# Block inverses of a chunked delta rule, cut into four quarters instead of two halves

## The reference

```python
q, k, v = (silu(conv4(x @ W.T)) for W in (Wq, Wk, Wv))
beta = sigmoid(x @ Wb.T)
A = where(tri_strict, -(kb @ k.T), 0)          # kb = k * beta, 32x32 per chunk
T = solve_triangular(eye - A, eye, lower=True)
u, w = T @ v, T @ kb                           # then a scan over the chunks
local = fir3(v), fir15(v), fir63(v)            # per channel filters
o = p0*local_s + p1*local_m + p2*local_l + p3*delta_out + p4*v
```

## Time and profile before

| | |
|---|---|
| median of 3 timed runs | 2339.09 us (2338.53 to 2339.15) |
| the profiled execution, own time | 2325.58 us |
| its span, first to last instruction | 2323.8 us |
| stage 1 (project) | from 0 to 359.2 us of the span |
| stage 2 (weights_fir) | from 359.2 to about 576 us |
| busy share over the whole span | PE 90%, DVE 50%, ACT 37%, POOL 23% |

### The profile page before, as it was taken

How to read it: one execution, slowest core, us unless ns; L and a number is a source line. 1 busy time by engine, 2 the same in 40 slices (tenths; PEclk the granted TensorE clock), 3 DMA queues, 4 the chain that set the end, 5 groups by cost and what they waited for, 6 DMA issues and landing times.

```text
span 2323.8 us, 41398 instructions
## 1 busy us (share of the span) xinstructions
PE 2086.2 (90%) x16936; PEld 1766.6 (76%) x16936; DVE 1157.7 (50%) x1819; ACT 864.5 (37%) x1406; POOL 533.1 (23%) x563
## 2 busy tenths in 40 slices
PE   7888873776899888779999999999999999999998
PEld 5776763676777777658888888888888888888886
DVE  5777768963477767732343244234324323432332
ACT  4445541110233333234344344434434433443442
POOL 1112787875455554500000000000000000000000
PEclk9999996798799999989999999999999999999999
DMA  5766666776999999500000000000000000000000
GB/s 162 203 189 178 185 206 173 245 248 235 217 226 207 208 206 204 132 27 1 19 19 1 19 19 1 19 19 19 1 19 19 1 19 19 19 1 19 19 1 18
DMA packets 247007, 217.02 MB, mean 93 GB/s; under 512 B 159042, under 2 KB 210754, under 8 KB 242242
## 3 DMA queue, kind: packets, MB, share of 16 engines
q1 hardware_dynamic: 234562, 184.30, 31.0%
q10 hardware_dynamic: 12288, 30.41, 4.5%
HBM read 130.52 MB, written 84.15 MB: 92 GB/s over the span
## 4 chain that ended last, share of the span: by engine, by line
PE 55%; issue 1%; DVE 1%; ACT 1%; DMA 0%; POOL 0%; DVEq 0%; SPq 0%; ACTq 0%; POOLq 0%
PE B L1573 49%; PE O L1600 5%; PE T L1531 1%; DVE yb L1706 0%; ACT gate L1645 0%; DMA x<-x_s 0%; DVE stats L1737 0%; ACT L1645 0%; DVE z L1732 0%; DVE z L1728 0%; DVE xl L1686 0%; DVE z L1751 0%; ACT xh L1633 0%; POOL rstd L1787 0%; DVEq L1701 0%
## 5 line engine op out<-in xcount | busy, mean ns | idle before, releaser
L1573 PE MATMUL B<-act1l,wr 128*128 128x512 f32 x1024 | 398.5, 389 | 0.0
L1573 PE MATMUL B<-act0h,wr 128*128 128x512 f32 x1024 | 398.3, 389 | 0.0
L1573 PE MATMUL B<-act0l,wr 128*128 128x512 f32 x1024 | 398.3, 389 | 0.0
L1573 PE MATMUL B<-act1h,wr 128*128 128x512 f32 x1024 | 398.3, 389 | 0.0
L1659 ACT ACTIVATE yb<-B,scol 128x512 f32<-128x512 f32 x256 | 176.2, 688 | 581.1 <-PE B L1573 581.1
L1694 DVE TENSOR_TENSOR act0l<-yb,act0h 128x512 fp32r<-128x512 f32 x256 | 176.1, 688 | 378.0 <-ACT act0h L1662 375.8
L1784 POOL TENSOR_TENSOR rstd<-mv,ln_eps 128x4 f32<-128x4 f32 x16 | 3.2, 199 | 1303.5 <-DVE mv L1745 1303.5
L453 DVE SCALAR_TENSOR_TENSOR acc<-proj,taps,acc 128x512 f32<-128x512 f32 x288 | 214.7, 750 | 84.8 <-ACT acc L399 76.3
L1694 DVE TENSOR_TENSOR act1l<-yb,act1h 128x512 fp32r<-128x512 f32 x128 | 88.7, 693 | 295.4 <-ACT act1h L1662 295.4
L1573 PEld LDWEIGHTS B<-act0h,wr 128*128 128x128 f32 x1024 | 192.3, 188 | 39.9
L1573 PEld LDWEIGHTS B<-act1h,wr 128*128 128x128 f32 x1024 | 192.3, 188 | 39.9
(11 more groups left out here) (169 smaller groups left out, 3213.7 us busy)
## 6 DMA issues: line engine op xcount, KB each, us to landing
qk_s<-yT SPq DMA_DIRECT2D x16, 1024.0 KB, 6.2
kk_s<-kfull SPq DMA_DIRECT2D x16, 1024.0 KB, 6.4
qk<-qk_s SPq DMA_DIRECT2D x32, 512.0 KB, 6.5
wraw<-in_ffn_w ACTq DMA_DIRECT2D x32, 352.0 KB, 6.5
toe<-in_toe_short ACTq DMA_DIRECT2D x32, 320.0 KB, 7.4
xt<-in_xt SPq DMA_DIRECT2D x16, 524.0 KB, 4.3
k_s<-ktok SPq DMA_DIRECT2D x16, 512.0 KB, 7.2
v_s<-vtok SPq DMA_DIRECT2D x16, 512.0 KB, 3.2
```

The costliest lines, as they stand in the source:

```text
L1573: last = nc.tensor.matmul(B[slot % 4][:, :], w, part, start=(k == 0 and i == 0), stop=(k == kts - 1 and i == len(parts) - 1))
```

## The change

The matrices are cut into four parts of four steps each, two slots per part (s is 2). GpSimd makes three of the parts, each while the next four steps are projected, and the last six columns of the third in stage 2. VectorE makes the fourth part in stage 2, five instructions to four groups, over 48 groups. The scales are therefore made three times in stage 1, each at half the size. The inverses are stored in four parts. All loops over steps in stage 1 on TensorE, ScalarE and VectorE are written out.

```diff
-EARLY_COLS = {10: (1, 5), 11: (5, 9), 12: (9, 12), 13: (12, 15), 14: (15, 18), 15: (18, 21), 16: (21, 25)}
+PARTS = 4
+PART_STEPS = STEPS // PARTS
+PSLOTS = SLOTS // PARTS
+PGRP = GRP // PARTS
+
+EARLY_COLS = {6: (0, 1, 8), 7: (0, 8, 14), 8: (0, 14, 20), 9: (0, 20, 31),
+              10: (1, 1, 8), 11: (1, 8, 14), 12: (1, 14, 20), 13: (1, 20, 31),
+              14: (2, 1, 8), 15: (2, 8, 15), 16: (2, 15, 25)}
 EARLY_END = 25
...
-                    early = isinstance(t, int) and t == EARLY_STEPS + 1
+                    c = t // PART_STEPS - 1
+                    early = c in range(PARTS - 1) and t % PART_STEPS == 1
                     if early:
-                        pe.wait_ge(gam0_done, 1)
-                        nc.tensor.transpose(gam_ps, gam0[:, :, :, :].rearrange("p t r s -> p (t r s)"), ident).then_inc(gam0_turned, 1)
+                        pe.wait_ge(gam0_done, c + 1)
+                        turn_scales(nc, gam_ps, gam0, ident).then_inc(gam0_turned, 1)
                     turn(lambda hh, b: yT[p][:, KT + hh, b * P:b * P + P]).then_inc(ktok_ready, 1)
                     if early:
-                        pe.wait_ge(gam0_out, 2)
+                        pe.wait_ge(gam0_out, 2 * c + 2)
...
                 step(0, 0, 0, False)
-                with dve.Fori(0, EARLY_STEPS // 2) as i:
-                    step(i * 2 + 1, 1, i, True)
-                    step(i * 2 + 2, 0, i, True)
-                first_scales()
-                with dve.Fori(EARLY_STEPS // 2, STEPS // 2 - 1) as i:
-                    step(i * 2 + 1, 1, i, True)
-                    step(i * 2 + 2, 0, i, True)
-                step(STEPS - 1, 1, STEPS // 2 - 1, True)
+                for t in range(1, STEPS):
+                    step(t, t % 2, (t - 1) // 2, True)
+                    if t % PART_STEPS == 0:
+                        first_scales(t // PART_STEPS - 1)
...
                     if t in EARLY_COLS:
-                        first, end = EARLY_COLS[t]
+                        c, first, end = EARLY_COLS[t]
+                        sub = Substitution(nc.gpsimd, keep, c, keep["outer0"])
                         if first == 1:
...
-                        early_columns(nc, pool, sub, keep, first, end)
+                        early_columns(pool, sub, keep, c, first, end)
+                        if end == CH - 1:
+                            early_rows(pool, sub, keep, c)
+                    if t % PART_STEPS == 1 and t > 1:
+                        c = t // PART_STEPS - 1
+                        if c < PARTS - 1:
+                            blocks_there(pool, keep, c)
+                            Substitution(nc.gpsimd, keep, c, None).zero_above().then_inc(keep["sub_link"], 1)
...
-        COLS = CH - 2
-
-        D_OUT, T_OUT = {2: 0, 18: 1}, {4: 0, 20: 1}
-
-        TURNS = {2: 0, 16: 1}
+        OPS = 2 * (CH - 2)
+        SUB_END = OPS * 4 // 5
+
+        D_OUT, T_OUT = {2: 0, 6: 1, 12: 2, 27: 3}, {4: 0, 8: 1, 14: 2, 28: 3}
+
+        TURNS = {2: 0, 5: 1, 11: 2, 26: 3}
...
                 for n in range(NGRP):
                     weigh(n)
-                    if n < COLS:
-                        link(sub.outer_product(n + 1))
-                        link(sub.update(n + 1))
-                    if n == COLS:
+                    if n < SUB_END:
+                        for i in range((n * 5 + 3) // 4, (n * 5 + 8) // 4):
+                            link(sub.update(i // 2 + 1) if i % 2 else sub.outer_product(i // 2 + 1))
+                    if n == SUB_END:
 
                         dve.wait_ge(upper_zero, 1)
-                        sub.scaled_rows().then_inc(inv_done[1], 1)
+                        sub.scaled_rows().then_inc(keep["inv_done"][1], 1)
```

More of the change, by code:

```diff
@@ L184, in project @@
         gates = side[0][:, 0:BATCH * 24].rearrange("p (b n) -> p b n", b=BATCH)
[L185 removed]
+        gam_ps = side[0][:, P:P + PGRP]
         norms = side[1][:, 0:BATCH * HEADS].rearrange("p (b n) -> p b n", b=BATCH)
@@ L346, in step @@
                             after[cb](t - 1, 1 - p)
-                step(0, 0, 0, False)
-                with pe.Fori(0, EARLY_STEPS // 2) as i:
-                    step(i * 2 + 1, 1, i, True)
[L351 to L354, removed]
-                    step(i * 2 + 1, 1, i, True)
-                    step(i * 2 + 2, 0, i + 1, True)
-                step(STEPS - 1, 1, STEPS // 2 - 1, True)
+                for t in range(STEPS):
+                    step(t, t % 2, t // 2, t > 0)
                 for piece in after.values():
@@ L420, in _ @@
                 step(0, 0, 0, False, True)
[L421 to L432, removed]
-                    step(i * 2 + 1, 1, i, True, False)
+                for t in range(1, STEPS):
+                    step(t, t % 2, (t - 1) // 2, True, t < 2)
+                    if t % PART_STEPS == 0:
+                        c = t // PART_STEPS - 1
+                        act.wait_ge(small_out, t + 1)
+                        if c:
+                            act.wait_ge(gam0_done, c)
+                        nc.scalar.activation(ebeta[:, :, :], raw[:, c * NE:c * NE + NE, NGATE:NGATE + HEADS], ACT.Exp,
+                                             scale=-1.0).then_inc(exp0_done, 1)
                 keys_out(STEPS - 1, 1, STEPS // 2 - 1)
@@ L555, in early_columns, with early_rows, by_matrix @@
         sub.outer_product(j).then_inc(keep["sub_link"], 1)
-        pool.wait_ge(keep["sub_link"], 2 * j + 1)
+        pool.wait_ge(keep["sub_link"], c * SUB_LINKS + 2 * j + 1)
         sub.update(j).then_inc(keep["sub_link"], 1)
+def early_rows(pool, sub, keep, c):
+    pool.wait_ge(keep["sub_link"], (c + 1) * SUB_LINKS)
+    sub.scaled_rows().then_inc(keep["inv_done"][0], 1)
+def by_matrix(nc, gam, half):
+    for par in range(2):
+        last = nc.vector.tensor_copy(gam[:, :, par, :],
+                                     half.rearrange("p (v b) (k r) -> p v r (b k)", v=2 * PART_STEPS, r=2)[:, :, par, :])
+    return last
@@ L560, in weights_fir, with turn_scales @@
+def turn_scales(nc, out, gam, ident):
+    for rows in HALVES:
+        last = nc.tensor.matmul(out[rows, :], gam[rows, :, :, :].rearrange("p t r s -> p (t r s)"), ident[rows, rows],
+                                start=True, stop=True)
+    return last
 def weights_fir(nc, sems, io, keep):
@@ L775, in _ @@
                 dve.wait_ge(to_root, 1)
-                link(nc.vector.tensor_tensor(half[:, :, :], ssk[:, :, :], beta[:, :, :], ALU.mult))
+                link(nc.vector.tensor_tensor(half[:, :, :], ssk[:, LAST, :], beta[:, :, :], ALU.mult))
                 link(nc.vector.reciprocal(half[:, :, :], half[:, :, :]))
-                for par in range(2):
-                    last = nc.vector.tensor_copy(gam[:, :, par, :], streams(half[:, :, :])[:, :, par, :])
-                last.then_inc(gam_done, 1)
+                by_matrix(nc, gam, half[:, :, :]).then_inc(gam_done, 1)
                 link(nc.vector.tensor_scalar(eps[:, :], prm[:, NGATE + HEADS:NGATE + 2 * HEADS], 0.0, 0.2, ALU.max, ALU.min))
```

154 lines of the change are left out of this document (79 added, 75 removed).

## The result

The change makes the kernel slower. In the comparison its median is 2403.18 us (2395.79 to 2405.16, 4 runs), that of the kernel before 2338.81 us (2328.75 to 2339.15, 4 runs): a ratio of 1.028 with a 95% interval of 1.0245 to 1.0316. The forecast was 2330 us. (The ratio is formed from the executions of one comparison, without slow ones, so it can differ by some tenths of a percent from the quotient of the two medians.)

What follows compares the result with a forecast made beforehand. In stage 2's filters VectorE bounds the first 30 groups, then TensorE where DMA lets it; GpSimd holds stage 1's barrier. Stage 1 +25, prologue -4, filters -31, tail +1 give -9 us: 2330 us, range 2313 to 2348.

Steps and rivals of the forecast that it cites:

- DMA, the step that failed: Stage 2 loop: bytes stay, 8 us added for bunched loads, 142 us against 173.15, -31 us; bounds -45 and -12.
- the DMA rival: Stage 2 loop: loads get 43 us a head, loop 155 to 161 us, kernel about 2346 us; chance 0.16.
- The tail: Behind the filters: the fourth part's stores end nearer to the barrier, +1 us, bounds 0 and 3.
- The filters: Stage 2's 64 groups: 100 us for 48 groups, 134 us in all before DMA's 8 us; -31 us.
- The prologue: Start of stage 2: VectorE's chain shortens, first `weigh` at about 390.7 instead of 394.85, -4 us; bounds 0 and -6.
- Stage 1: All terms added in stage 1 together: +25 us, forecast range +18 to +29.
- The barrier: End of stage 1: GpSimd's last columns stand ahead of the barrier, +12.6 us, bounds +10 and +15.
- The passages: Stage 1: three passages of the scales at 4.3 us each for one of 4.9, +8 us; bounds +5 and +10.
- contention: Stage 1, later two passages: VectorE's short instructions take turns with GpSimd's, +5 us for both; bounds 0 and 8.
- GpSimd late: Stage 1, steps 10 and 14: GpSimd 4.3 us late against 4.5 slack, +1 us together, bounds 0 and 8.
- The loops: Stage 1: six loops written out, an estimate of -2 us, bounds 0 and -3.
- The sum: Whole kernel: 25 - 4 - 31 + 1 = -9 us, 2316.6 us profiled, carried over to 2330 us timed.

Runs made afterwards that it cites:

- run 1: The changed kernel with each store of inverses cut in two, 64 groups outermost in each half; 2313.99 us against 2326.63, ratio 0.997.
- run 2: The kernel before with only its stores made narrow, each cut at row 82 into 82 and 46 rows; 2389.38 us, ratio 1.027.
- run 8: Run 6's kernel with the unturned inverses of the first two parts (1 MB) stored already in stage 1; 2302.55 us, ratio 0.9918.
- run 9: The kernel before with only VectorE's half spread over 48 groups, its stores and turn following the later end; 2310.3 us, ratio 0.9912.
- run 6: Run 1's kernel with six columns of GpSimd's third part moved behind the barrier to stage 2; 2306.24 us, 0.9891; taken again 2304.91 us, 0.9912.
- run 10: Run 9's kernel with stage 1's loops on TensorE, ScalarE and VectorE written out; 2301.57 us, ratio 0.9886.
- run 4: The changed kernel with one of three stores per part, that of the unturned blocks, cut into halves; 2357.26 us, ratio 1.0141.
- run 5: The changed kernel, stores still narrow, the first three parts' moved behind the loads of the heads; 2383.47 us, ratio 1.0267.
- run 3: The kernel before with its stores cut evenly at row 64, as many DMAs as run 2; 2326.08 us, ratio 1.0014.

## Why the prediction was wrong, step by step

**DMA, the step that failed.** "The bytes stay", and they were given the old rate: the upper bound of the loop, 161 us, was made from heads in which all 16 engines worked. The pattern of the stores had changed. Their bytes stay, but run at 51 to 52 GB/s, and the loop was 215.9 us, 55 beyond the bound. Runs 1 and 2 show the cause from both sides: with it taken from the change 65 us of loop come back, and with it put into the kernel before 39 are lost. No rival held it either: the one on DMA (2346 us) had all engines' bandwidth short, and no case had a store that keeps SP from issuing.

**The tail,** +1 us with a bound of 3, was +17.6. It is the same step: the last part's stores at two sixteenths. Mended, the piece is 6.8 us, as before, so the term would then have been 0.

**The filters apart from that** gained, as forecast, but less. Run 1 gives 150.9 us on the table's measure, 23.9 less than before, against the forecast's 31, within its range of 12 to 45. VectorE was priced too high: its 60 instructions of the substitution took 39.4 us together, where the forecast had 33 and 22 more for meeting GpSimd's adds. The 8 us that were added for bunched loads were too few. DMA shares are 1.00 and 1.02 in the second and third heads. The third head takes 43.07 us at 287 GB/s although no inverse is stored in it, just what it took before. That was the premise of the DMA rival, whose loop was 155 to 161 and which was to decide from 151 on; run 1 lies at that line. TensorE waits 21.9 us in all for `toe` in run 1 and 4.1 for VectorE. Shares and waits both speak for DMA as what holds the mended filters; it is not shown, for run 8, with 1 MB less in the loop, was not faster. (The forecast's lower bound calls 128 us TensorE's; that is the figure of the DMA share, and TensorE alone would be 64 x 1.76 = 113.) The forecast set the number down to fewer and narrower instructions on VectorE; by run 9 the spreading alone gives 16 us with the wide ones.

**The prologue,** -4 us: measured -3.5 in the kernel after and -5.0 in run 1 (first `weigh` 32.2 and 30.7 us into the stage, forecast 31.5). Right.

**Stage 1,** +25 us: measured +26.5, and +19.6 in run 1. Its terms:

- The barrier, +12.6: measured +11.4. GpSimd's last instruction holds it, and VectorE is idle for 17.0 us (forecast 18), as these rows of the kernel after show:

```profile
384.41 0.89 POOL L159 TENSOR_TENSOR tri<-tri,outer 128x336 f32<-128x336 f32 x1
...
385.64 1.06 DVE L791 TENSOR_SCALAR rq<-raw 128x256 f32<-128x256 f32 x1 [16.98 <-PEq L220]
```

  Run 6 tests it: with 12 instructions fewer behind the last key squares the seam is 12.2 us earlier, and the kernel faster: 2306.24 against 2313.99 us, at ratios whose intervals don't overlap.
- The passages, +8, contention, +5, and GpSimd late, +1, together +14: measured +16.9, and +10.6 in run 1. Three passages in run 1 cost 6.1, 4.7 and 4.7 us over plain steps, where one of full width cost 4.9, and 6.0 in run 10. The forecast left out what part of that is clock. In the second step of the one passage before, the granted clock was 0.93 and the same matmuls were busy 1.6 us longer; every passage of every run has at least one step below 1.00, and halving the elementwise parts did not take that away:

```profile
203.25:226.55 23.30, 19.39 (x162) 15.80 (x162) 16.17 (x23) 10.87 (x19) 6.52 (x33) 0.93 0.60 171
226.55:246.73 20.18, 17.76 (x161) 14.44 (x162) 15.84 (x23) 10.32 (x17) 15.83 (x15) 1.00 0.64 197
```

  Contention was 1.15 us in a passage where the engines meet, and not 2.5; in run 1 the instruction that took 1.17 us in both later passages took 0.23. The stall for late key squares was 0.4 us. So three terms were off and nearly made up for each other. The rule of the Trainium skill, SBUF — State Buffer, Who interferes with whom, is borne out by the 1.17 us against 0.23: the product waited for the whole of GpSimd's instruction. The term of 8 that the forecast drew from it is not: one instruction and two copies were longer, the reciprocal was not.
- The kernel after and run 6 have 6 us more in the third passage. Its two steps in the kernel after, and the same two in run 1:

```profile
271.47:297.67 26.20, 21.19 (x161) 17.08 (x161) 19.27 (x30) 13.15 (x20) 16.61 (x14) 0.84 0.47 152
297.67:322.89 25.22, 21.92 (x165) 17.63 (x166) 14.98 (x21) 10.66 (x19) 23.45 (x33) 0.83 0.54 158
```

```profile
270.87:292.74 21.87, 17.81 (x161) 14.45 (x162) 16.64 (x28) 13.04 (x20) 16.73 (x14) 1.00 0.57 182
292.74:315.94 23.20, 19.85 (x165) 15.67 (x166) 16.48 (x24) 10.78 (x19) 21.41 (x25) 0.93 0.57 171
```

  The same matmuls are busy for 43.1 us instead of 37.7, at a granted clock of 0.84 instead of 1.00 and 0.93. The list of instructions in stage 1 is the same in both kernels. The profiles with 0.83 to 0.84 there (the kernel after, run 6 twice, run 8) are all ones in which the product waited 1.17 us in both later passages; in runs 1 and 4 it didn't wait, and the third passage took 45.1 us. So contention may cost far more than its 1.15 us. But in run 5 the product waited too, and the third passage took 46.4 us. What lowers the clock in one execution and not in the other stays open.
- The loops, -2, a guess that no row carried: measured -2.0 to -2.5, and run 10 has plain steps of 20.18 us where run 9 has 20.27 to 20.60.

**The sum.** On stages 1 and 2 the mended change (run 1) begins stage 3 at 567.08 us against 576.40, -9.3 us; the forecast's sum was -9. Its ratio of 0.997 makes 2332 us of 2338.8, and the ratio of the two medians (2313.99 to 2326.63) 2326; the forecast was 2330. That it comes so close is luck: against run 1 stage 1 was forecast 5 us too dear and the filters 7 us too good, errors of opposite sign. The work that was moved was read nearly right, and the transfer that was only rewritten was not read at all.

**The change against its parts.** Four parts instead of two make the loop 8 us shorter (158.9 in run 9, 150.9 in run 1) and the prologue 5, and stage 1 is 18 us longer (378.7 against 360.7). On those profiles they don't pay: run 9 begins stage 3 at 562.1 us and run 1 at 567.1. With the short tail of run 6 it is 565.0 and 562.6. But run 6 has the loops of stage 1 written out as well, and the run to hold beside it is run 10, at 557.2: 5 to 8 us earlier with two parts. The timed ratios (0.9886 and 0.9912 in one comparison) can't tell the two apart.

## What to carry to other kernels

When a change touches a transfer, compare its access pattern with the old one and not only its bytes: which dimension is outermost on both sides, and into how many DMA engines its size divides. In a trace, stretches with every engine idle and a DMA share of a small whole number of sixteenths (here 0.12 to 0.13) point to it, as does an issue that holds its queue for ten microseconds and more; look then at what is queued behind it, and at how late the loads arrive that have been issued. And test the cheapest part of a change by itself: here the order of VectorE's instructions alone held two thirds of the gain in the filters (16 of 24 us) and changed nothing in the stage ahead.

## What the runs showed that was not expected

- Stores at two sixteenths of the engines move 51 to 52 GB/s, some 26 per engine, and their issues hold the queue: up to 18.61 us, against 0.58 us for the store of twice the size before. It is not every issue. Of the last part's three, the first two took 0.54 us each and the third, right behind the second, 11.65. That fits a bound on how much may be outstanding at a DMA engine, but it is only argued; no run tests it.
- The waits cost clock as well: TensorE's granted clock was 0.76 over the filters of the kernel after, at its lower level (0.50) in the idle stretches, and 0.91 in run 1.
- With the stores mended, the filters' DMA share times length is 137 us (0.91 of 150.9), where the kernel before had 128 and run 9 has 130. Nearly the same bytes took more of the engines' time with more in flight; the runs don't say why.
- Stages 3 and 4, whose instructions no run touches, took from 1730.5 us (run 1) to 1758.4 us (run 9), with 1747.4 before. So one profile can't carry a verdict on the whole that is smaller than this spread of 28 us. The seams are steadier: run 6's two profiles begin stage 3 2.4 us apart, the kernel before and run 3, which differ only in the cut of the stores, 3.0 us. Differences of a few microseconds between seams are still near that.
